# The last-but-one tile of a convolution and quantised dense layer: second pass on ScalarE and an accumulating DMA in place of one VectorE pass, and another order for the tail

## The reference

```python
out = conv(x, weight, groups=4, K=9) + ctx[:, :, None] + bias[None, :, None]
xq = fake_quant(out, bits=8, axis=-1)      # round(v / s) * s, s = max|row| / 127
kq = fake_quant(kernel, bits=8, axis=0)
y = einsum('bsd,df->bsf', xq, kq) + fake_quant(bias, bits=16)
return x + fake_quant(y, bits=8, axis=-1)
```

## Time and profile before

| | us |
|---|---|
| median of 3 runs | 250.9 |
| all three | 253.15, 250.19, 250.9 |
| the profiled execution's own time | 250.28 |
| its span, first to last instruction | 248.2 |
| PE busy | 233.9 (94%) |
| DVE busy | 206.7 (83%) |
| POOL busy | 191.1 (77%) |
| ACT busy | 183.9 (74%) |

### The profile page before, as it was taken

One profiled execution on the slowest core, in us unless ns is written; L12 is line 12 of the kernel. 1 busy time (PEld: TensorE's weight loads), 2 busy tenths in 40 slices (PEclk: granted clock), 3 DMA queues, 4 the chain that ended last, 5 costly groups with the idle time before them and its releaser, 6 DMA issues.

```text
span 248.2 us, 3979 instructions
## 1 busy us (share of the span) xinstructions
PE 233.9 (94%) x1306; PEld 148.8 (60%) x1306; DVE 206.7 (83%) x421; ACT 183.9 (74%) x182; POOL 191.1 (77%) x135
## 2 busy tenths in 40 slices
PE   7799999999999999999999999999999999999920
PEld 4478577756666666566656666665666666656400
DVE  3799897867888898778997897899798979877894
ACT  4589788866777877577598769867897975966652
POOL 4674270339999999889849986995999599989980
PEclk9999999999999999999999999999999999999995
DMA  6996600193227789996889999999989999968938
GB/s 222 399 414 251 254 1 3 17 343 111 86 24 228 171 203 342 200 364 172 170 202 282 193 282 253 248 216 356 209 224 325 241 367 204 284 116 203 417 140 333
DMA packets 16388, 56.29 MB, mean 227 GB/s; under 512 B 2288, under 2 KB 2416, under 8 KB 16368
## 3 DMA queue, kind: packets, MB, share of 16 engines
q1 hardware_dynamic: 11808, 42.08, 46.8%
q0 software_dynamic: 3744, 13.63, 30.9%
q10 hardware_dynamic: 816, 0.33, 0.5%
HBM read 39.26 MB, written 16.78 MB: 226 GB/s over the span
## 4 chain that ended last, share of the span: by engine, by line
PE 87%; DVE 6%; DMA 2%; issue 1%; POOL 1%; ACT 0%; SPq 0%; DVEq 0%
PE dense_ps L691 42%; PE conv_ps L635 35%; PE turn_ps L671 6%; PE small_ps L661 2%; DMA xwin<-x_windows 2%; PE dense_ps L711 1%; DVE a_int L924 1%; DVE y_max L950 1%; DVE small_ps L895 1%; POOL x_lo L324 1%; PE conv_ps L691 1%; DVE y L890 1%; DVE last_max L975 0%; DVE k_max L846 0%; ACT x_hi L441 0%
## 5 line engine op out<-in xcount | busy, mean ns | idle before, releaser
L691 PE MATMUL dense_ps<-kq,a_t 128*128 128x512 bf16 x496 | 115.5, 379 | 0.0
L324 POOL TENSOR_TENSOR x_lo<-xwin,x_hi 128x1032 fp32r<-128x1032 f32 x32 | 81.8, 2571 | 30.1 <-ACT x_hi L441 25.6
L332 POOL TENSOR_TENSOR y<-y,bq 128x512 f32<-128x512 f32 x60 | 81.4, 1448 | 10.9 <-DVE y L881 10.9
L691 PEld LDWEIGHTS dense_ps<-kq,a_t 128*128 128x128 bf16 x496 | 47.2, 100 | 49.0 <-issue 2.0
L895 DVE TENSOR_REDUCE small_ps<-conv_ps 128x8 f32<-128x1024 f32 x32 | 39.3, 1227 | 17.2 <-PE conv_ps L635 17.2
L501 ACT ACTIVATE y_int<-y,y_inv 128x1024 int16<-128x1024 f32 x31 | 35.6, 1148 | 18.0 <-DVE y_inv L936 17.9
L881 DVE SCALAR_TENSOR_TENSOR y<-dense_ps,row_scale,k_scale_b 128x512 f32<-128x512 f32 x58 | 43.1, 745 | 6.0 <-PE dense_ps L691 6.0
L486 ACT CAST a_t<-turn_ps 128x1024 bf16<-128x1024 int16 x32 | 32.3, 1010 | 20.6 <-PE turn_ps L671 20.5
L635 PE MATMUL conv_ps<-x_hi,w_hi 128*128 128x512 f32 x128 | 40.1, 435 | 1.4 <-ACT x_hi L441 1.4
L924 DVE TENSOR_TENSOR a_int<-conv_ps,inv 128x1024 int16<-128x1024 f32 x32 | 39.2, 1224 | 0.0
L441 ACT CAST x_hi<-xwin 128x1032 fp32r<-128x1032 f32 x32 | 33.7, 1053 | 6.4 <-DMA xwin<-x_windows 6.4
(11 more groups left out here) (67 smaller groups left out, 154.6 us busy)
## 6 DMA issues: line engine op xcount, KB each, us to landing
xwin<-x_windows SPq DMA_DIRECT2D x32, 516.0 KB, 6.6
out<-y SPq DMA_DIRECT2D x30, 512.0 KB, 4.2
y<-x_rows POOLq DMA_DIRECT2D x26, 512.0 KB, 7.4
k_raw<-ffn_kernel SPq DMA_DIRECT2D x8, 512.0 KB, 7.8
x_sb<-x_rows SPq DMA_DIRECT2D x6, 512.0 KB, 7.3
w_raw<-taps SPq DMA_DIRECT2D x2, 256.0 KB, 3.3
b_row<-ffn_bias SPq DMA_DIRECT2D x1, 512.0 KB, 10.0
out<-x_sb SPq DMA_DIRECT2D x1, 512.0 KB, 3.1
```

What stands on the lines that cost most here:

```text
L324: pool.tensor_tensor(x_lo[:, at].rearrange("p n b -> p (n b)"), xwin[:, t % XWIN, :], x_hi[:, at].bitcast(F32).rearrange("p n b -> p (n b) ...
L332: pool.tensor_tensor(y[:, t % YRING, half(h)], y[:, t % YRING, half(h)], bq[:, half(h)], ALU.add).then_inc(s["biased1" if h else "biased_e ...
L691: mm = pe.matmul(dense_bank(t, h), a_t[:, t % LEVELS, q].rearrange("b j o -> b (j o)"), kq[:, q, half(h)], start=(q == 0), stop=(q == Q - 1))
```

## The change

Tile 30 joins the tiles that take `x` by an accumulating DMA: `by_dma` holds for it, `finish` and its semaphore go away, `quantise(30)` runs both ScalarE passes, and `add_x(30)`, the last instruction on GpSimd, issues the DMA. Its `x` is no longer loaded into `x_sb`. `store(30)` waits for that DMA. The lists of all five engines after the loop are written in another order.

```diff
         def by_dma(t):
-            return t < 26
+            return t < 26 or t == LAST - 1
...
             def store(t):
-                if t == LAST - 1:
-                    sp.wait_ge(s["finished"], 1)
-                    sp.dma_start(out[t], x_sb[:, nth_pool(t) % XRING, :]
-                                 ).then_inc(stored[t % YRING], 16)
-                    return
                 if by_dma(t):
                     sp.wait_ge(x_added[t % YRING], nth_dma(t))
...
 # SyncE, the end of its list
-            load_x(LAST)
-            store(LAST - 2)
-            store(LAST - 3)
+            store(LAST - 8)
+            store(LAST - 3)
+            store(LAST - 2)
             store(LAST - 1)
             store_last(sp, 0)
...
 # GpSimd, the end of its list
             add_x(LAST - 3)
             add_x(LAST - 2)
+            add_x(LAST - 1)
...
 # ScalarE, the end of its list
-            round_y(LAST - 1)
+            quantise(LAST - 1)
             quantise_last()
             store_last(act, 1)
...
 # TensorE, the end of its list
             dense(LAST - 1, 1)
+            dense(LAST - 1, 0)
             turn_levels(LAST)
-            dense(LAST - 1, 0)
             dense(LAST, 1)
             dense(LAST, 0)
...
 # VectorE, the end of its list
-            scale_half(LAST, 1)
             out_scale(LAST - 1)
             scale_half(LAST, 0)
+            scale_half(LAST, 1)
+            add_bias(LAST, 0)
+            maximum_last(0)
             add_bias(LAST, 1)
-            add_bias(LAST, 0)
             maximum_last(1)
-            maximum_last(0)
             out_scale_last()
-            finish(LAST - 1)
             add_x_last()
```

More of the change, by code:

```diff
@@ L119, in build @@
             "a_made", "dense_made0", "dense_made1", "scaled0", "scaled1", "biased0", "biased1", "biased_last", "biased_early", "scaled_act", "scaled_pool", "biased_pool",
-            "y_max_made", "y_scale_made", "y_inv_made", "y_rounded", "y_dequantised", "added", "finished", "last_max", "last_rounded", "last_made")}
+            "y_max_made", "y_scale_made", "y_inv_made", "y_rounded", "y_dequantised", "added", "last_max", "last_rounded", "last_made")}
         w_in = [sem(f"w_in{i}") for i in range(2)]
@@ L275, in _ @@
             load_xwin(LAST - 3)
+            load_xwin(LAST - 2)
             load_x(LAST - 5)
-            load_xwin(LAST - 2)
-            store(LAST - 12)
+            load_xwin(LAST - 1)
             load_x(LAST - 4)
-            load_xwin(LAST - 1)
-            store(LAST - 11)
             load_xwin(LAST)
+            store(LAST - 13)
             load_x(LAST - 3)
             load_x(LAST - 2)
+            load_x(LAST - 1)
+            store(LAST - 12)
+            store(LAST - 5)
+            store(LAST - 11)
+            store(LAST - 6)
+            load_x(LAST)
+            store(LAST - 4)
+            store(LAST - 7)
             store(LAST - 10)
-            store(LAST - 13)
-            store(LAST - 5)
-            load_x(LAST - 1)
+            store(LAST - 9)
             store(LAST - 8)
[L290 to L293, removed]
-            load_x(LAST)
+            store(LAST - 3)
             store(LAST - 2)
-            store(LAST - 3)
             store(LAST - 1)
@@ L389, in _ @@
                         add_x(t)
-            add_x(LAST - 12)
             add_bias(LAST - 9, 1)
-            add_x(LAST - 11)
             split(LAST - 4)
             add_bias(LAST - 8, 0)
+            split(LAST - 3)
             add_bias(LAST - 8, 1)
+            split(LAST - 2)
             add_bias(LAST - 7, 0)
+            add_x(LAST - 12)
+            add_bias(LAST - 6, 0)
+            add_x(LAST - 11)
             add_bias(LAST - 7, 1)
-            split(LAST - 3)
-            add_x(LAST - 10)
-            split(LAST - 2)
             split(LAST - 1)
             add_bias(LAST - 6, 1)
+            add_x(LAST - 10)
             add_x(LAST - 9)
-            add_bias(LAST - 6, 0)
-            split(LAST)
             add_x(LAST - 8)
@@ L408, in _ @@
             add_bias(LAST - 5, 1)
+            split(LAST)
+            add_x(LAST - 7)
             add_bias(LAST - 4, 0)
             add_bias(LAST - 4, 1)
-            add_x(LAST - 7)
             add_x(LAST - 6)
+            add_bias(LAST - 3, 1)
+            add_x(LAST - 5)
             add_bias(LAST - 3, 0)
-            add_x(LAST - 5)
             scale_and_add(LAST - 2, 0)
-            add_bias(LAST - 3, 1)
             add_x(LAST - 4)
@@ L567, in _ @@
                     quantise(t)
+            round_x(LAST - 4)
             seed(LAST - 5)
-            round_x(LAST - 4)
-            quantise(LAST - 11)
+            round_x(LAST - 3)
             take_levels(LAST - 7)
-            quantise(LAST - 10)
-            round_x(LAST - 3)
             seed(LAST - 4)
-            quantise(LAST - 9)
             take_levels(LAST - 6)
             round_x(LAST - 2)
+            quantise(LAST - 11)
+            quantise(LAST - 10)
+            seed(LAST - 3)
+            quantise(LAST - 9)
+            take_levels(LAST - 5)
+            round_x(LAST - 1)
             quantise(LAST - 8)
-            seed(LAST - 3)
-            round_x(LAST - 1)
-            take_levels(LAST - 5)
+            seed(LAST - 2)
+            quantise(LAST - 7)
             take_levels(LAST - 4)
+            seed(LAST - 1)
             round_x(LAST)
-            seed(LAST - 2)
-            seed(LAST - 1)
-            quantise(LAST - 7)
+            take_levels(LAST - 3)
             quantise(LAST - 6)
-            take_levels(LAST - 3)
             quantise(LAST - 5)
+            seed(LAST)
             take_levels(LAST - 2)
-            seed(LAST)
+            quantise(LAST - 4)
             scale_rows(LAST - 2, 0)
-            quantise(LAST - 4)
             take_levels(LAST - 1)
             scale_rows(LAST - 2, 1)
+            quantise(LAST - 3)
             take_levels(LAST)
-            quantise(LAST - 3)
             quantise(LAST - 2)
-            round_y(LAST - 1)
+            quantise(LAST - 1)
             quantise_last()
@@ L773, in _ @@
             turn_levels(LAST - 7)
+            dense(LAST - 8, 0)
             dense(LAST - 8, 1)
-            dense(LAST - 8, 0)
+            spread_max(LAST - 6)
             conv(LAST - 5)
-            spread_max(LAST - 6)
-            dense(LAST - 7, 1)
+            turn_levels(LAST - 6)
             dense(LAST - 7, 0)
-            turn_levels(LAST - 6)
             spread_max(LAST - 5)
             conv(LAST - 4)
+            dense(LAST - 7, 1)
             dense(LAST - 6, 0)
+            turn_levels(LAST - 5)
+            spread_max(LAST - 4)
             dense(LAST - 6, 1)
-            spread_max(LAST - 4)
-            turn_levels(LAST - 5)
             conv(LAST - 3)
+            dense(LAST - 5, 0)
+            dense(LAST - 5, 1)
             turn_levels(LAST - 4)
-            dense(LAST - 5, 1)
             spread_max(LAST - 3)
-            dense(LAST - 5, 0)
             conv(LAST - 2)
+            turn_levels(LAST - 3)
+            dense(LAST - 4, 0)
             dense(LAST - 4, 1)
-            dense(LAST - 4, 0)
             spread_max(LAST - 2)
-            turn_levels(LAST - 3)
+            dense(LAST - 3, 0)
+            dense(LAST - 3, 1)
+            turn_levels(LAST - 2)
             conv(LAST - 1)
-            dense(LAST - 3, 0)
-            turn_levels(LAST - 2)
-            dense(LAST - 3, 1)
             dense(LAST - 2, 0)
@@ L952, in out_scale @@
                 scale_of(t)
[L954 to L960, removed]
             def add_x_last():
@@ L1041, in _ @@
             out_scale(LAST - 10)
-            scale_half(LAST - 8, 1)
-            out_scale(LAST - 9)
             scale_half(LAST - 8, 0)
             levels(LAST - 6)
+            scale_half(LAST - 8, 1)
             column_max(LAST - 5)
+            levels(LAST - 5)
+            out_scale(LAST - 9)
             scale_half(LAST - 7, 0)
+            column_max(LAST - 4)
+            scale_half(LAST - 7, 1)
+            scale_half(LAST - 6, 0)
             out_scale(LAST - 8)
-            scale_half(LAST - 7, 1)
-            levels(LAST - 5)
-            column_max(LAST - 4)
+            levels(LAST - 4)
             scale_half(LAST - 6, 1)
-            levels(LAST - 4)
-            scale_half(LAST - 6, 0)
+            out_scale(LAST - 7)
             column_max(LAST - 3)
-            out_scale(LAST - 7)
+            scale_half(LAST - 5, 0)
             scale_half(LAST - 5, 1)
@@ L1059, in _ @@
             out_scale(LAST - 6)
-            scale_half(LAST - 5, 0)
             column_max(LAST - 2)
-            scale_half(LAST - 4, 1)
             scale_half(LAST - 4, 0)
             out_scale(LAST - 5)
+            scale_half(LAST - 4, 1)
             levels(LAST - 2)
+            scale_half(LAST - 3, 1)
+            out_scale(LAST - 4)
             scale_half(LAST - 3, 0)
             column_max(LAST - 1)
-            out_scale(LAST - 4)
-            scale_half(LAST - 3, 1)
```

(2 more changed lines are left out.)

## The result

The changed kernel takes 253.05 us in the median of 16 runs (252.38 to 254.47); the kernel before, beside it, 250.58 in 16 (249.76 to 253.15). The ratio is 1.0081, 95% interval 1.0057 to 1.0105: slower by 2.0 us, which is within 2%. This ratio is not the quotient of the two medians, which are 2.5 us apart. The profiled execution took 252.58 with a span of 250.9.

The account below looks back on a forecast made before the run. TensorE bounds the kernel up to 230 us; then tile 30's path decides: DMA issued 240.4, landed 246.1, half 0 issued 246.5, landed 249.9, span 250.3. That is +2.1 on 250.28, 252.4, plus 0.3: 252.7 us (251.0 to 255.2).

Parts of the forecast that it names:

- the path of tile 30: Tile 30's DMA, then the stores waiting behind it on SyncE, set the end of the span at 250.3, 2.1 us later.
- TensorE's order: Tile 31's product, its cast no longer covered, starts at 234.9; TensorE idles about 1.3 us and ends 1.05 later.
- rival C: TensorE made to wait before 230 us by the new lists; one us lost there gives 253.7; chance 0.08.
- Issue of the DMA: On GpSimd, behind tile 29's addition, tile 30's accumulating DMA is issued at 240.4.
- Landing: Tile 30's accumulating DMA lands 5.7 us after issue, 5.2 and half a us for tile 29's store, at 246.1.
- rival B: Stores slow tile 30's accumulating DMA: time 255.2 with a landing of 8.2, 256.6 with 9.6; chance 0.22.
- the 8.2: Landing time in us of an earlier accumulating DMA, issued at 211.7 beside stores, taken as the slowed case.
- What is queued behind it: On SyncE, half 0 of tile 31 is issued at 246.5, lands after 3.4 at 249.9; span 250.3.
- Tile 31: Its chain's last store is issued at 245.4; with 3.1 and 0.4 it ends at 248.9, 1.4 before tile 30's end.
- A: Tile 30's DMA lands within 4.2 us in idle DMA engines, tile 31 decides: 250.9, not slower; chance 0.10.

Follow-up runs that it names:

- E1: The changed kernel without tile 30's accumulating DMA, so tile 30 leaves without its x: 250.5 us, ratio 0.998.
- E3: The changed kernel's order of the lists, with tile 30's end as in the kernel before (no accumulating DMA for it): 251.4 us, ratio 1.003.
- E5: The changed kernel with half 0 of tile 31 stored ahead of tile 30 on SyncE: 252.27 us, ratio 1.0056.
- E12: The changed kernel with tile 30's last DMA a plain copy of x and tile 29's store at the end of SyncE's list: 251.43 us, one run.
- E6: The changed kernel with tile 29's store moved behind tile 30's store and half 0 of tile 31: 254.19 us, ratio 1.0121.
- E2: The kernel before, in its old order, with only tile 30's end changed to the second ScalarE pass and accumulating DMA: 255.15 us, ratio 1.0152.
- E4: The changed kernel with tile 31's transpose moved back between the halves of tile 30's product on TensorE: 255.28 us, ratio 1.0138.
- E8: The changed kernel with tile 30's last DMA a plain copy of x, without the addition: 252.56 us, ratio 1.0061.
- E11: The kernel before with tile 28 stored ahead of 29, tile 30 taking both ScalarE passes and its x added by GpSimd: 251.14 us, ratio 1.0021.
- E10: The kernel before with tile 28 stored ahead of tile 29 on SyncE, run twice: 250.39 and 250.55 us, ratios 0.9981 and 1.0002.

## Why the prediction was right

It said 252.7 (251.0 to 255.2) by the path of tile 30, and 253.05 was measured. Against the kernel before it said 1.8 more, from a median of 250.9 in three runs; measured beside it are 2.0 by the ratio. The path and what waits on it were right, the price of the landing was half a us too low. Step by step:

- *TensorE's order.* Right: a gap of 1.1 to 1.3 released by the cast, the product 1.05 later by itself. The granted clock held at 1.00 through the gap. The measured 1.34 has 0.35 more: 0.12 from the start of the execution and 0.23 from 182 us on, where I had costed the rest of the order at nothing. The 0.23 is the same in E1, E3, E5 and E12, which keep this order; no single wait stands behind it, and it is all that rival C took.
- *Issue of the DMA.* 240.4 was said, 240.83 measured: the same 0.35, and 0.1.
- *Landing.* 5.7 was said, 6.2 measured. The mechanism was right, the size of the store's share was not: half a us was put down for tile 29's store, and E6 shows 1.0. That is rival B, in a small dose; the 8.2 did not come, but E2, with tile 28's store and an earlier half 1 under way, has 7.4, and E4, with an earlier half 1, 7.0.
- *What is queued behind it.* The half's issue 0.4 later was right, and E5 wins 0.8 by lifting it. Its landing of 3.4 was too long by 0.5, since it was taken from a row in which four stores drained together; here only tile 30's store was under way with it. It made up for the landing.
- *Tile 31.* The last store of its chain was said to leave at 245.4 and left at 245.79, the 0.35 again. E1 shows that this chain by itself ends 2.5 us before the changed kernel does; 1.4 was said, with 3.1 for the landing of a half that in E1 takes 2.1.
- *Rivals.* A needed a landing within 4.2; the accumulating DMA never came under 5.1 in any profile here. The Trainium skill's formula (DMA: Bandwidth & Descriptors, "Anatomy of one DMA — SWDGE (gpsimd) path") comes near for the plain copy: an estimate of 3.2 by it, 3.5 in E12. The accumulation adds 1.7 to that (5.2 in E6).

In the sum, the errors were +0.35 (TensorE), +0.1, +0.5 (landing), -0.5 (last half), +0.1 (end): 250.3 became 250.9. That the time came within 0.4 owes something to two of them cancelling, and that is luck.

What stays open is why an accumulation takes 1.6 to 1.7 us more for the same bytes; E8's theory T1 names a read of the destination, and no run took such a read away. Why the waits in the first 25 us of an execution vary was not tried either.

## What to carry to other kernels

Near the end of a program, price a DMA by issue to landing, not by the time of the engine that it relieves: here 1.28 us of VectorE were exchanged for 6.2 us of landing, plus everything that stood behind its wait in the same issue queue. In the middle the 26 accumulating DMAs do not show on the path: TensorE is full there, with 48.00 of 48 us from 182 to 230. For the last tiles of this kernel an engine's own addition is the cheaper way: in the old order the aligned span is 248.1 with GpSimd's addition (E11) and 252.4 with the DMA (E2), and some 0.4 of that is tile 28's earlier store (E10). Before comparing profiles by tenths, line them up at an instruction that the change cannot have moved.

## What the runs showed of the hardware

- 512 KB on GpSimd's DMA queue, from memory to SBUF, land after 3.5 us as a plain copy (E12) and 5.2 as an accumulating one (E6), when next to nothing else is under way; one store of 512 KB issued at the same time adds 1.0 to 1.1 to either, while that store itself lands after 2.7 beside the accumulating DMA (changed kernel) and 3.0 beside the plain copy (E8).
- VectorE's pass over 128x512 with two tensors in SBUF took 1.03 us in E11 when GpSimd added two tensors in SBUF during the first 0.5 us of it, and 0.74 without; this is one instruction in one profile. The Trainium skill (GPSIMD Engine Reference, "Key points") has the two engines share their SBUF interfaces, with contention for VectorE instructions that have two SBUF inputs; the row agrees.
- The start of an execution varies: tile 3's convolution began between 21.9 and 25.0 us in the 14 profiles of this study, and the time from there to tile 25's agrees within 0.02 us in all of them, 158.60 to 158.62. Part of the variation is the clock: it fell to its lower level for about 3.4 us in E4 and 6.8 us in E8, and in no other.
